# A gated feed-forward layer on one core: four of the twelve gate-up products on GpSimd, two of the gate conversions on VectorE

## The reference

```python
def act_qdq(x):                      # 16 bits, one scale for the whole tensor
    scale = jnp.maximum(jnp.max(jnp.abs(x)) / qmax, 1e-12)
    return jnp.clip(jnp.round(x / scale), -qmax - 1.0, qmax) * scale
...
x = act_qdq(x)
up = act_qdq(x @ lpbq_dequant(w_up).T)          # 2048 tokens x 768
gate = act_qdq(x @ lpbq_dequant(w_gate).T)
sig = fixed_qdq_u16(jax.nn.sigmoid(gate))
gate = act_qdq(gate * sig)
o = act_qdq(gate * up)
return o @ lpbq_dequant(w_down).T
```

## Time and profile before

| what | value |
| --- | --- |
| unprofiled runs | 898.75 us median (895.82 to 899.81) |
| profiled execution, first to last instruction | 909.3 us |
| TensorE busy in it | 849.0 us (93%) |
| VectorE / ScalarE / GpSimd busy | 618.8 / 504.3 / 161.1 us |
| mean granted TensorE clock | 0.972 |
| the changed stage, first conversion to the reduction of the twelve maxima | 830.55 to 861.04 us |

### The profile page before, as it was taken

The page is one execution under the profiler, slowest core; times in us unless marked ns, Lnnn a source line. Parts: engine busy times, 40 slices in busy tenths (PEclk is TensorE's granted clock), DMA queues, the critical chain, the costliest instruction groups (busy, mean ns, idle before and its releaser), DMA issues.

```text
span 909.3 us, 14428 instructions
## 1 busy us (share of the span) xinstructions
PE 849.0 (93%) x4542; PEld 474.4 (52%) x4543; DVE 618.8 (68%) x1207; ACT 504.3 (55%) x678; POOL 161.1 (18%) x283
## 2 busy tenths in 40 slices
PE   9999999999988999999968999999999989993398
PEld 6543333333468899999844433333334654441387
DVE  5898888888771222233248978888886578698942
ACT  4567777777731122222235667777777674597660
POOL 3241111111264000000151423000005303000000
PEclk9999999999999999999988999999999989997699
DMA  8898466654362111111469663333310000000011
GB/s 296 184 285 235 91 168 171 164 165 127 114 212 93 35 35 35 37 38 38 162 181 239 180 182 73 80 84 83 82 43 2 1 1 1 0 0 1 0 41 52
DMA packets 66558, 91.13 MB, mean 100 GB/s; under 512 B 24134, under 2 KB 50630, under 8 KB 66502
## 3 DMA queue, kind: packets, MB, share of 16 engines
q1 hardware_dynamic: 59196, 67.83, 29.0%
q0 software_dynamic: 5584, 19.93, 6.6%
q10 hardware_dynamic: 1728, 2.75, 0.8%
HBM read 62.64 MB, written 27.44 MB: 99 GB/s over the span
## 4 chain that ended last, share of the span: by engine, by line
PE 80%; DVE 8%; ACT 4%; issue 2%; DMA 2%; another core or an unknown queue 2%; SPq 1%; POOL 1%; DVEq 0%; ACTq 0%; POOLq 0%
PE PS L2197 13%; PE PS L2165 13%; PE PS L2186 12%; PE PS L2356 9%; PE PS L2422 8%; PE PS L2341 8%; PE PS L2443 5%; PE PS L2297 3%; PE PS L2148 1%; PE PS L2211 1%; PE PS L2128 1%; PE PS L2111 1%; PE PS L2175 1%; ACT BIG L1291 1%
## 5 line engine op out<-in xcount | busy, mean ns | idle before, releaser
L1571 DVE TENSOR_REDUCE MX<-PS 128x1 f32<-128x512 f32 x512 | 321.4, 684 | 44.3 <-PE PS L2165 43.6
L1148 ACT ACTIVATE Pt<-PS 128x1024 f32<-128x1024 f32 x256 | 248.1, 1021 | 101.6 <-PE PS L2186 100.7
L2165 PE MATMUL PS<-KSt,BIG 96*128 96x512 bf16 x512 | 175.4, 384 | 3.7 <-DVE bias_row L1458 2.7
L2186 PE MATMUL PS<-BIG,KSt 99*128 99x512 bf16 x512 | 150.5, 380 | 2.1 <-ACT Pt L1148 1.4
L2197 PE MATMUL PS<-Pt,VS 128*17 128x512 f32 x1024 | 137.0, 601 | 0.0
L2165 PEld LDWEIGHTS PS<-KSt,BIG 96*128 96x128 bf16 x512 | 40.6, 97 | 144.5 <-DVE MX L1571 87.3
L2341 PEld LDWEIGHTS PS<-KSt,Pt 128*128 128x128 f32 x736 | 85.6, 192 | 1.9 <-issue 0.8
L2341 PE MATMUL PS<-KSt,Pt 128*128 128x128 f32 x736 | 86.0, 275 | 0.7 <-issue 0.7
L1695 DVE COPY KSt<-PS 128x256 f32<-128x256 f32 x23 | 9.8, 425 | 111.1 <-PE PS L2328 111.1
L2422 PE MATMUL PS<-KSt,BIG 128*128 128x512 f32 x192 | 83.5, 596 | 0.0
L2186 PEld LDWEIGHTS PS<-BIG,KSt 99*128 99x128 bf16 x512 | 49.5, 98 | 56.3 <-ACT Pt L1148 4.9
(11 more groups left out here) (199 smaller groups left out, 1077.4 us busy)
## 6 DMA issues: line engine op xcount, KB each, us to landing
qk_parts<-BIG SPq DMA_DIRECT2D x64, 192.0 KB, 3.7
BIG<-in_w POOLq DMA_DIRECT2D x12, 1024.0 KB, 5.6
BIG<-qk_parts SPq DMA_DIRECT2D x32, 192.0 KB, 3.3
KSt<-qk_parts SPq DMA_DIRECT2D x32, 192.0 KB, 3.8
v_rows<-BIG SPq DMA_DIRECT2D x8, 544.0 KB
VS<-v_rows SPq DMA_DIRECT2D x32, 136.0 KB, 3.0
BIG<-qk_parts SPq DMA_DIRECT2D x32, 128.0 KB, 3.8
KSt<-qk_parts SPq DMA_DIRECT2D x32, 128.0 KB, 3.9
```

Source lines behind the costliest of these rows:

```text
L1148: act.activation(PP[:, 2 * (kc % 2) + half, :, :].rearrange("p h t -> p (h t)"), ST[half], ACT.Exp, scale=DK ** -0.5).then_inc(exp_done, 1)
L1571: dve.tensor_reduce(MX[:, g % 2, i % TB, i // TB:i // TB + 1], ring(i), AX.X, ALU.max, negate=True).then_inc(max_taken, 1)
L2165: pe.matmul(ring(i), QS[0:ROWS, g, h, qc * P:(qc + 1) * P], KS[0:ROWS, g, h, :], start=True, stop=True).then_inc(max_done, 1)
L2186: last = pe.matmul(ST[half][:, i * S:(i + 1) * S], KS[0:ROWS + PARTS, g, h, kc * P:(kc + 1) * P], QS[0:ROWS + PARTS, g, h, :], start=True, ...
```

## The change

GpSimd makes products 1, 4, 7 and 10 (`PRODUCTS_ON_POOL`). For each it turns the gate's int16 piece into floats (into a slot of the `sig` buffer, which the sigmoid has left), then up's int16 piece into floats (over the float up piece that has been read), waits for both, and multiplies them into the gate piece. VectorE makes the other eight products and all twelve maxima; the maximum of a product of GpSimd is taken two to three steps later in its list. VectorE also converts gate pieces 0 and 6 itself (`GATES_ON_DVE`); ScalarE makes the other 22 conversions. The waits on products and on gate conversions look up which engine made them (`product_taken`, `gates_ready`). The threshold of TensorE's first `keep_busy` falls from 22 to 18.

```diff
+        PRODUCTS_ON_POOL = (1, 4, 7, 10)
+        GATES_ON_DVE = (0, 6)
+        def product_taken(eng, i):
+            if i in PRODUCTS_ON_POOL:
+                eng.wait_ge(pool_prod, on_pool(i) + 1)
+            else:
+                eng.wait_ge(prod_done, PIECES + 1 + i - on_pool(i) + 1)
+        def gates_ready(eng, i):
+            if i in GATES_ON_DVE:
+                eng.wait_ge(gate_own, GATES_ON_DVE.index(i) + 1)
+            else:
+                eng.wait_ge(gate_scaled, i - sum(j < i for j in GATES_ON_DVE) + 1)
...
+            for k, i in enumerate(PRODUCTS_ON_POOL):          # GpSimd
+                whole = halves(Q["sig"][:, k % SIGS, :])
+                gates_ready(gp, i)
+                gp.tensor_scalar(whole, whole_piece(i + SIGS), 1.0, 1.0, ALU.mult, ALU.mult).then_inc(pool_float, 1)
+                gp.wait_ge(up_int, i + 1)
+                gp.tensor_scalar(piece(Q["up"], i), ups_piece(i), 1.0, 1.0, ALU.mult, ALU.mult).then_inc(pool_float, 1)
+                gp.wait_ge(pool_float, 2 * k + 2)
+                gp.tensor_tensor(piece(Q["gate"], i), whole, piece(Q["up"], i), ALU.mult).then_inc(pool_prod, 1)
...
             for i in range(PIECES):                           # ScalarE
-                wait(act, prod_done, PIECES + 1 + i - SIGS + 1 if i >= SIGS else 0)
-                act.activation(whole_piece(i + SIGS), piece(Q["gate"], i), ACT.Copy,
-                               scale=sc[:, F_2:F_2 + 1]).then_inc(gate_scaled, 1)
+                if i not in GATES_ON_DVE:
+                    if i >= SIGS:
+                        product_taken(act, i - SIGS)
+                    act.activation(whole_piece(i + SIGS), piece(Q["gate"], i), ACT.Copy,
+                                   scale=sc[:, F_2:F_2 + 1]).then_inc(gate_scaled, 1)
                 scale_up(i)
...
+            def gate_whole(i):                                # VectorE
+                dve.wait_ge(scales, 3)
+                if i >= SIGS:
+                    product_taken(dve, i - SIGS)
+                dve.tensor_scalar(whole_piece(i + SIGS), piece(Q["gate"], i), sc[:, F_2:F_2 + 1], None,
+                                  ALU.mult).then_inc(gate_own, 1)
+            def top(i):
+                product_taken(dve, i)
+                return dve.tensor_reduce(cmx[:, i:i + 1], piece(Q["gate"], i), AX.XY, ALU.max,
+                                         apply_absolute_value=True)
+            gate_whole(GATES_ON_DVE[0])
+            for i in range(PIECES):
+                if i not in PRODUCTS_ON_POOL:
+                    gates_ready(dve, i)
                     dve.wait_ge(up_int, i + 1)
+                    dve.tensor_tensor(piece(Q["gate"], i), whole_piece(i + SIGS), ups_piece(i),
+                                      ALU.mult).then_inc(prod_done, 1)
+                if i + 1 in GATES_ON_DVE[1:]:
+                    gate_whole(i + 1)
+                if i > 0 and i - 1 not in PRODUCTS_ON_POOL:
+                    top(i - 1)
+                if i - 3 in PRODUCTS_ON_POOL:
+                    top(i - 3)
+            top(PRODUCTS_ON_POOL[-1])
+            last = top(PIECES - 1)
...
-            pe.wait_ge(prod_done, 2 * PIECES - 2)
+            pe.wait_ge(prod_done, 2 * PIECES - 2 - len(PRODUCTS_ON_POOL))
```

More of the change, by code:

```diff
@@ L274, in build_program @@
         gate_scaled = sem("gate_scaled")
+        gate_own = sem("gate_own")
+        pool_float = sem("pool_float")
+        pool_prod = sem("pool_prod")
         o_scaled = sem("o_scaled")
@@ L466, in pairs_at, with on_pool @@
             return range(i - 2, i - 1) if PAIRS_SOON + 1 < i <= PIECES else ()
+        def on_pool(i):
+            return sum(j < i for j in PRODUCTS_ON_POOL)
+        def product_taken(eng, i):
[8 more added lines that the diff above has]
+                eng.wait_ge(gate_scaled, i - sum(j < i for j in GATES_ON_DVE) + 1)
         def tokens(i):
@@ L1270, in scale_up @@
                 act.wait_ge(scales, 4)
-                wait(act, prod_done, PIECES + 1 + i - UPS + 1 if i >= UPS else 0)
+                if i >= UPS:
+                    product_taken(act, i - UPS)
                 act.activation(ups_piece(i), piece(Q["up"], i) if i < PIECES - 1 else pair_banks(i), ACT.Copy,
@@ L1854, in _ @@
             next_scale(0, sc[:, S_X:S_X + 1], S_U, F_U).then_inc(scales, 1)
[L1856 to L1859, removed]
-                    dve.wait_ge(up_int, i + 1)
[L1861 to L1865, removed]
+            def gate_whole(i):
[12 more added lines that the diff above has]
+                    gates_ready(dve, i)
+                    dve.wait_ge(up_int, i + 1)
+                    dve.tensor_tensor(piece(Q["gate"], i), whole_piece(i + SIGS), ups_piece(i),
[8 more added lines that the diff above has]
+            last = top(PIECES - 1)
             link(dve, last)
```

## The result

The changed kernel takes 902.58 us (median of six runs, 902.21 to 904.54) against 897.94 (six runs, 895.72 to 900.62): ratio 1.0052, 95% interval 1.0032 to 1.0071, some 4.6 us or 0.5% slower. That is inside the predicted range of 896.2 to 903.2, 3.4 us above the 899.2 predicted, and on the slower side of what I called "the same". It is outside the 898.3 to 900.5 that the prediction gave as its forecast's own range; the wider range holds it only through the room left for rival 2.

What follows compares the result with a forecast made beforehand. VectorE bounds the stage, then TensorE's down projection. The shorter list's -1.98 us and the hold-ups' 0.53 + 0.69 + 0.84 give +0.1; the clock's +0.3 makes +0.4, 899.2 us, range 896.2 to 903.2.

Steps and rivals of the forecast that it cites:

- rival 2: GpSimd's conversions from int16 are dear, from 1.2 us up: +3.6 to +5.8, 902.7 to 904.9 us; chance 0.18.
- U0's start to T11's start: ScalarE's first up conversion to VectorE's last maximum: 28.4 us forecast, 26.3 without holds, over 32 with dear conversions.
- The list without holds: VectorE's shortened list with no hold-up between engines: last maximum starts at 857.83 against 859.81, 1.98 us earlier.
- The hold-ups: VectorE's two-input SBUF products and GpSimd's operations wait whole for each other: losses 0.53 + 0.69 + 0.84 us.
- rival 1: VectorE's int16 products are not held by GpSimd, or never meet it: -1.98 + 0.3, 897.1 us; chance 0.17.
- P2, P5, P6 and P9: VectorE's products of pieces 2, 5, 6 and 9: held by GpSimd, losing nothing, 0.53, 0.69 and 0.84 us.
- M: GpSimd's two-input product of one piece, 1,024 floats: 1.96 us, from a line through rows.
- C7, D7 and M7: GpSimd's two conversions and product for piece 7: first delays VectorE's product 6 by 0.69 us, others lie under maxima.
- this cliff: At conversions of 1.20 us GpSimd's product 10 falls ahead of VectorE's product 9: losses 5.54 us, hence +3.6.
- The clock: TensorE idle 7.3 us before the spread, so spread and 8 matmuls behind it at 1.2 GHz: +0.3 us.
- rival 3: TensorE's clock comes back late, as at 742, slowing the down projection: +0.1 + 2.1, 901.0 us; chance 0.10.
- g5, g8 and g11: ScalarE's gate conversions 5, 8 and 11: their waits on GpSimd's products 1, 4 and 7 end before ScalarE comes.

Runs made afterwards that it cites:

- experiment 8: Changed kernel with GpSimd making three products (1, 4, 7) and VectorE nine: stage 31.56 us, span 900.6 us, one execution.
- experiments 3 to 6: On the changed kernel: up operand in PSUM, stage 27.91 us; fused form in SBUF, 33.39. On the kernel before: GpSimd products nobody awaits, 39.96; memsets instead, 29.55.
- experiment 9: Changed kernel with TensorE's matmuls on ones waiting for VectorE's product 9, not 6: stage 33.38 us, reduction to last matmul 45.45 us.

## Why the prediction was right, and where it was off

**In short:** the mechanism was right, and so was "the same"; the forecast of +0.4 us was not, with +4.6 measured. That the time fell inside 896.2 to 903.2 is in part luck: the room above 900.5 was made for dear conversions, which didn't happen, and something else filled it. The prediction's own sign says so: from U0's start to T11's start it gave 28.4 us for the forecast and over 32 for rival 2, and about 32.0 were measured (818.89 to 850.9).

**The bound** was read rightly: VectorE sets the end of the stage in every kernel here, and what the stage loses the kernel loses, as long as the clock holds; in experiment 8 it didn't.

**The list without holds,** -1.98 us: with the products freed by PSUM the stage came to 27.91, -1.64, of which the longer PSUM form on ScalarE takes 0.24 (1.193 us a conversion, against 1.133, so that P3 starts 7.82 us after the scale, at 833.72, where U3 would have let it start 7.58 after it). Right to about 0.1 us.

**The hold-ups** exist for int16 products, and are whole: rival 1 is out by the changed kernel's own rows and by experiments 3 to 6. They fell on P2, P5, P6 and P9 as written, but also on P8 and G6, and the one on P2, put at nothing, cost 0.32 us.

**The conversion from int16** costs 1.03 to 1.04 us, where I had taken 1.05. Rival 2's cause is out, though its size, +3.6 at a conversion of 1.2 us, is nearly the one measured.

**The step that was mis-sized** is the price of M: 1.96 us "on that line" between 256 and 1,536 floats. It takes 2.34 to 2.35. Its 0.39 us, four times, would be 1.6 us; what they did is to put C7, D7 and M7 so late that M10 falls ahead of P9 and C7 ahead of G6, and the holds come to 5.67 us in place of 2.06 (0.53 + 0.69 + 0.84). The prediction knew this cliff, but hung it on the conversion alone; laid out again by its own rules with M at 2.35, the stage comes out at +3.7 us, an estimate, and at +1.3 already with M at 2.05, so its +0.1 stood at an edge. The range was built with the bounds of the conversion alone. The prediction had weighed one other price for M, 2.25, from the Trainium skill's GPSIMD Engine Reference, section "3.1 Elementwise — side-by-side cycle accounting", and given +1.5 for it. Here the Trainium skill's figure was nearer than my line through the rows. The long rows of that line, L934's, are of another kind, with one number for each block of 32 as the second operand. With M cut to 1.94 us the stage took 29.75, 0.20 over the kernel before, against +0.1 predicted: the sum holds once the term is right.

**The clock:** +0.3 taken, +0.2 measured in this comparison; the loss of rival 3 did not happen in the profiled run of the changed kernel, and did in that of experiment 8. The row on which rival 3 was built was read too simply: at 734 to 735 the granted clock is still 1.00, as TensorE starts again; it was lost at about 735.4 and came back at about 742.3. So that row, too, shows a clock that falls behind a restart, not one that takes 7.8 us to come back after a restart at 1.2 GHz.

**ScalarE** was to wait at none of g5, g8 and g11, and did not: its conversions start 1.04 us apart to the end (840.72 for the last).

## What to carry to other kernels

Before work is moved from VectorE to GpSimd, list which of VectorE's remaining instructions read two operands from SBUF, or scale from SBUF to SBUF: these and GpSimd's reads exclude each other, and the freed time can all go there. Put one operand in PSUM, or let GpSimd's long operations fall under reductions; and price the longest GpSimd operation from a row with the same operands, with both bounds, because with holds the loss isn't proportional: 0.4 us more per operation cost 3.6 us here.

## What the runs showed of the hardware

- A VectorE product with one input in PSUM and one in SBUF kept its 1.22 us beside GpSimd's two-input product (2.356 us), where the same product with both inputs in SBUF took up to 3.37. The Trainium skill's SBUF — State Buffer, section "Who interferes with whom", says that the second SBUF input is what contends; the runs agree. The same section of the Trainium skill says that a GpSimd instruction that only writes doesn't contend; here, too, the runs agree: twenty memsets of 0.951 us left the stage at 29.55 us.
- GpSimd's float product of two full operands took 2.35 us for 1,024 elements and 1.94 for 832; its sum of two full operands took, in the kernel before, 0.726 for 256: on one line with the products, about 2.1 ns an element. L934, 1,536 elements in 2.780 us, lies 0.65 us under that line; that the repeated operand is the reason is argued, not shown.
- The clock can be full at a restart and fall behind it: in experiment 8 it was lost 1.4 us after TensorE had begun again and returned 6.8 us later, though TensorE was at work but for 0.55 us, and the down projection grew by 2.3 us (43.99 against 41.69 in experiment 9).
